# One Softplus in place of four operations and a sum, in the bidirectional scan of a four-layer kernel on one core

## The reference

```python
x_dbl = jnp.einsum('bkdl,kcd->bkcl', xs, x_proj_w)
dts, Bs, Cs = jnp.split(x_dbl, [R, R + N], axis=2)      # R = 8, N = 1
dts = jnp.einsum('bkrl,kdr->bkdl', dts, dt_w)
dt = jax.nn.softplus(dts + dt_b[None, :, :, None])
A = -jnp.exp(A_logs).reshape(K, Cm, N)
a = jnp.exp(dt[..., None] * A[None, :, :, None, :])      # the decay
b = (dt * u)[..., None] * Bs                             # the input term
h[l] = a[l] * h[l-1] + b[l]                              # the scan
ys = h * Cs + Ds * u
y02 = ys[:, 0] + ys[:, 2, :, ::-1]
y13 = ys[:, 1] + ys[:, 3, :, ::-1]
```

## Time and profile before

| what | value |
|---|---|
| median of the runs | 3650.93 us |
| profiled execution | 3652.96 us |
| its span in the profile | 3651.0 us |
| mean granted clock of PE | 0.937 |
| PE / DVE / ACT / POOL busy, of the span | 80 / 67 / 65 / 30% |

### The profile page before, as it was taken

One profiled execution on the slowest core, in us unless ns is written; L12 is line 12 of the kernel. 1 busy time (PEld: TensorE's weight loads), 2 busy tenths in 40 slices (PEclk: granted clock), 3 DMA queues, 4 the chain that ended last, 5 costly groups with the idle time before them and its releaser, 6 DMA issues. The chain is left out here.

```text
span 3651.0 us, 45449 instructions
## 1 busy us (share of the span) xinstructions
PE 2936.3 (80%) x17500; PEld 1593.8 (44%) x17500; DVE 2437.7 (67%) x2565; ACT 2368.8 (65%) x2681; POOL 1101.4 (30%) x612
## 2 busy tenths in 40 slices
PE   3688876969969877778996888776998788769699
PEld 2344335435534434434553433443555344354355
DVE  5787657865579657676466964768636886576761
ACT  2888545468689745437778864644868977454484
POOL 0236103642025500463103530146310453025430
PEclk9999998989999999899998999988999999989899
DMA  2001473500200157440020034643002005564101
GB/s 67 18 1 40 121 199 118 161 9 1 73 23 1 53 141 208 118 119 9 0 91 5 1 93 123 200 132 91 9 9 87 0 0 142 139 182 135 41 1 52
DMA packets 137227, 274.91 MB, mean 75 GB/s; under 512 B 17139, under 2 KB 93622, under 8 KB 137014
## 3 DMA queue, kind: packets, MB, share of 16 engines
q1 hardware_dynamic: 137014, 272.01, 26.7%
HBM read 194.07 MB, written 77.88 MB: 74 GB/s over the span
## 5 line engine op out<-in xcount | busy, mean ns | idle before, releaser
L1499 DVE SCALAR_TENSOR_TENSOR work<-region,cols,work 128x768 f32<-128x768 f32 x288 | 373.3, 1296 | 8.4 <-ACT work L902 3.3
L678 POOL TENSOR_TENSOR region<-region 128x768 f32<-128x768 f32 x96 | 225.4, 2352 | 350.6 <-ACT region L862 344.6
L1017 PE MATMUL psum<-region,m_fc 128*128 128x384 f32 x768 | 282.6, 491 | 11.8 <-ACT work L969 11.8
L1017 PE MATMUL psum<-region,m_cen 128*128 128x384 f32 x384 | 159.7, 541 | 158.8 <-DVE region L1613 60.9
L1270 PE MATMUL psum<-work,m_fc 128*128 128x384 f32 x768 | 282.3, 491 | 0.0
L654 POOL TENSOR_TENSOR work<-work,region 128x768 f32<-128x768 f32 x96 | 174.5, 1818 | 211.5 <-DVE work L1429 211.5
L642 POOL TENSOR_TENSOR work<-work 128x768 f32<-128x768 f32 x48 | 102.1, 2130 | 442.6 <-ACT work L783 416.1
L220 DVE SCALAR_TENSOR_TENSOR region<-region,cols 128x768 f32<-128x768 f32 x192 | 223.9, 1166 | 12.3 <-POOL region L678 8.3
L969 ACT ACTIVATE work<-psum,cols 128x768 f32<-128x768 f32 x192 | 173.1, 901 | 87.6 <-PE psum L1017 82.9
L1017 PE MATMUL psum<-work,m_avg 128*128 128x384 f32 x576 | 216.9, 500 | 16.0 <-ACT work L824 8.0
L1416 DVE SCALAR_TENSOR_TENSOR work<-region,cols,work 128x768 f32<-128x768 f32 x144 | 195.7, 1379 | 40.9 <-POOL work L642 37.5
(11 more groups left out here) (234 smaller groups left out, 7530.5 us busy)
## 6 DMA issues: line engine op xcount, KB each, us to landing
work<-scratch_cpe SPq DMA_DIRECT2D x192, 196.0 KB, 4.1
work<-scratch_dwc SPq DMA_DIRECT2D x192, 196.0 KB, 4.2
work<-scratch_lepe SPq DMA_DIRECT2D x192, 196.0 KB, 4.1
region<-in_tab_ch SPq DMA_DIRECT2D x48, 768.0 KB, 5.9
region<-in_x SPq DMA_DIRECT2D x48, 384.0 KB, 3.5
region<-in_tab_tok SPq DMA_DIRECT2D x48, 384.0 KB, 3.2
out<-work SPq DMA_DIRECT2D x48, 384.0 KB, 2.5
scratch_cpe<-region SPq DMA_DIRECT2D x44, 392.0 KB, 4.7
```

The source lines that it names most:

```text
L678: g.tensor_tensor(chain_tile(conv, n, p), chain_tile(conv, n - 1, p), chain_tile(conv, n, p), ALU.add).then_inc(tap_done[n], 1)
L1017: last = pe.matmul(psum[:, bank + s, 0:HC], weights[:, :], moving(s), start=(n == 0), stop=(n == len(terms) - 1))
L1499: v.scalar_tensor_tensor(out=by_row(tile(acc + p)), in0=prow(k, b, *TAPS[n]), scalar=tap_weight(conv, TAPS[n]), in1=by_row(tile(acc + p)), ...
```

## The change

Softplus becomes one ACT operation, `ACT.Softplus`, from PSUM to the tile. It is in another table set than Exp, so blocks are handled in pairs: load the one set, two Softplus, load the other, two decays. DVE's `step_size` goes. The banks are shared out anew: dt has only banks 0 and 1, B has banks 2 and 3 for even blocks and 4 and 5 for odd ones, C stays in 6 and 7. PE's stages become an order of six entries over pairs. DVE's stages all have lag 0. POOL issues `du` ahead of `add_y`. The backward outputs go to tiles 8 and 9 instead of 4 and 5, so that DVE waits for `add_y` two blocks back, where ACT's decay did.

```diff
-        bu_flat = psum[:, 4:6, :].rearrange("p a c -> p (a c)")[:, 0:BLK]
+        bu_flat = [psum[:, 2 + 2 * p:4 + 2 * p, :].rearrange("p a c -> p (a c)")[:, 0:BLK] for p in range(2)]
...
-                    g.tensor_tensor(y, y, tile(4 + p), ALU.add).then_inc(c["y"], 1)
-
-                chained(g, NB, [(2, add_y), (0, du)])
+                    g.tensor_tensor(y, y, tile(8 + p), ALU.add).then_inc(c["y"], 1)
+
+                chained(g, NB, [(0, du), (2, add_y)])
...
-                def soft(sweep, b, p):
+                def soft(sweep, g, _):
 
                     c = c_sets[sweep]
-                    a.wait_ge(c["dt"], done(i, b))
-                    scanned(a, i, sweep, "decay", b, 2)
-                    scanned(a, i, sweep, "du", b, 2)
-                    a.activation(halves(tile(p)), pair(2 * p), ACT.Abs, bias=col(f"l1_dtb{sweep}")).then_inc(c["abs"], 1)
-                    a.wait_ge(c["abs"], done(i, b))
-                    a.activation(tile(p), tile(p), ACT.Exp, scale=-1.0).then_inc(c["exp"], 1)
-                    a.activation(pair(2 * p), pair(2 * p), ACT.Relu, bias=col(f"l1_dtb{sweep}")).then_inc(c["relu"], 1)
-                    a.wait_ge(c["exp"], done(i, b))
-                    a.activation(tile(p), tile(p), ACT.Ln, bias=col("one")).then_inc(c["log"], 1)
-
-                def decay(sweep, b, p):
+                    a.preload_act_table_set("softplus")
+                    for p in range(2):
+                        b = 2 * g + p
+                        a.wait_ge(c["dt"], done(i, b))
+                        scanned(a, i, sweep, "decay", b, 2)
+                        scanned(a, i, sweep, "du", b, 2)
+                        a.activation(halves(tile(p)), pair(0), ACT.Softplus, bias=col(f"l1_dtb{sweep}")).then_inc(c["step"], 1)
+
+                def decay(sweep, g, _):
 
                     c = c_sets[sweep]
-                    a.wait_ge(c["step"], done(i, b))
-                    if sweep == 0 or is_first(b) or (isinstance(b, int) and b == 1):
-                        scanned(a, i, sweep, "hc", b, 2)
-                    else:
-                        a.wait_ge(c["y"], done(i, b - 2))
-                    a.activation(tile(4 + p), tile(p), ACT.Exp, scale=col(f"l1_A{sweep}")).then_inc(c["decay"], 1)
-
-                a.preload_act_table_set("natural_log_exp_and_others")
-                chained(a, NB, [(2, decay), (0, soft)])
+                    a.preload_act_table_set("exp_and_others")
+                    for p in range(2):
+                        b = 2 * g + p
+                        a.wait_ge(c["step"], done(i, b))
+                        scanned(a, i, sweep, "h", b, 2)
+                        a.activation(tile(4 + p), tile(p), ACT.Exp, scale=col(f"l1_A{sweep}")).then_inc(c["decay"], 1)
+
+                chained(a, NB // 2, [(0, soft), (0, decay)])
...
-                def dt(sweep, b, p):
-                    scanned(pe, i, sweep, "step", b, 2)
-                    product(2 * p, [(w_dt[sweep], flat_rows(2, sweep_block(sweep, b)))]).then_inc(c_sets[sweep]["dt"], 1)
...
+                def dt(p):
+                    def stage(sweep, g, _):
+                        b = 2 * g + p
+                        scanned(pe, i, sweep, "step", b, 1)
+                        product(0, [(w_dt[sweep], flat_rows(2, sweep_block(sweep, b)))]).then_inc(c_sets[sweep]["dt"], 1)
+                    return stage
+
+                def of_B(p):
...
+                        scanned(pe, i, sweep, "h", b, 2)
...
+                def of_C(p):
...
+                        scanned(pe, i, sweep, "hc", b, 1)
+                        product(6, [(w_C[sweep], flat_rows(2, sweep_block(sweep, b)))]).then_inc(c_sets[sweep]["C"], 1)
+                    return stage
 
                 all_done(pe, i, b_act)
-                chained(pe, NB, [(3, bc), (0, dt)])
+                chained(pe, NB // 2, [(1, of_C(0)), (0, dt(0)), (1, of_B(1)), (0, dt(1)), (1, of_C(1)), (0, of_B(0))])
...
-                    v.tensor_tensor(halves(tile(p)), halves(tile(p)), pair(2 * p), ALU.add).then_inc(c["step"], 1)
...
-                    y = flat(3, b) if sweep == 0 else tile(4 + p)
+                    if sweep == 1:
+                        v.wait_ge(c["y"], done(i, b - 2))
+                    y = flat(3, b) if sweep == 0 else tile(8 + p)
...
-                chained(v, NB, [(3, input_term), (3, scan), (3, outputs), (1, step_size)])
+                chained(v, NB, [(0, input_term), (0, scan), (0, outputs)])
```

More of the change, by code:

```diff
@@ L258, in build @@
             c_sets.append({k: signal(f"c{d}_{k}", o) for k, o in (
-                ("dt", "p"), ("B", "p"), ("C", "p"), ("abs", "a"), ("exp", "a"), ("relu", "a"), ("log", "a"), ("step", "v"),
-                ("decay", "a"),
+                ("dt", "p"), ("B", "p"), ("C", "p"), ("step", "a"), ("decay", "a"),
                 ("du", "g"), ("bu", "v"), ("h", "v"), ("hc", "v"), ("y", "g")) if d + k != "fy"})
@@ L1085, in middle, with stage @@
             def middle(i, following_runs):
-                def dt(sweep, b, p):
-                    scanned(pe, i, sweep, "step", b, 2)
-                    product(2 * p, [(w_dt[sweep], flat_rows(2, sweep_block(sweep, b)))]).then_inc(c_sets[sweep]["dt"], 1)
[L1090 to L1098, removed]
+                def dt(p):
[5 more added lines that the diff above has]
+                def of_B(p):
+                    def stage(sweep, g, _):
+                        b = 2 * g + p
+                        whole = flat(2, sweep_block(sweep, b))
+                        scanned(pe, i, sweep, "h", b, 2)
+                        pe.matmul(bu_flat[p][:, 0:BANK], w_B[sweep][:, :], whole[:, 0:BANK], start=True, stop=True)
+                        pe.matmul(bu_flat[p][:, BANK:BLK], w_B[sweep][:, :], whole[:, BANK:BLK], start=True, stop=True)\
+                            .then_inc(c_sets[sweep]["B"], 1)
+                    return stage
+                def of_C(p):
+                    def stage(sweep, g, _):
+                        b = 2 * g + p
+                        scanned(pe, i, sweep, "hc", b, 1)
+                        product(6, [(w_C[sweep], flat_rows(2, sweep_block(sweep, b)))]).then_inc(c_sets[sweep]["C"], 1)
+                    return stage
                 all_done(pe, i, b_act)
-                chained(pe, NB, [(3, bc), (0, dt)])
+                chained(pe, NB // 2, [(1, of_C(0)), (0, dt(0)), (1, of_B(1)), (0, dt(1)), (1, of_C(1)), (0, of_B(0))])
                 def yc(b, p):
@@ L1434, in input_term @@
                     v.wait_ge(c["B"], done(i, b))
-                    v.tensor_tensor(bu_flat, tile(2 + p), bu_flat, ALU.mult).then_inc(c["bu"], 1)
+                    v.tensor_tensor(bu_flat[p], tile(2 + p), bu_flat[p], ALU.mult).then_inc(c["bu"], 1)
                 def scan(sweep, b, p):
@@ L1443, in scan @@
                     way = (lambda ap: ap) if sweep == 0 else (lambda ap: ap[:, ::-1])
-                    v.tensor_tensor_scan(way(tile(6 + p)), way(tile(4 + p)), way(bu_flat), initial=start,
+                    v.tensor_tensor_scan(way(tile(6 + p)), way(tile(4 + p)), way(bu_flat[p]), initial=start,
                                          op0=ALU.mult, op1=ALU.add).then_inc(c["h"], 1)
```

## The result

The changed kernel took 3593.72 us (median of 4 runs, 3584.61 to 3595.31), the kernel before 3650.68 in the runs beside it. The ratio is 0.9837, with a 95% interval of 0.9822 to 0.9851: 57 us or 1.6% faster. The forecast was 3588.5 with a range of 3566 to 3628. The profiled execution was the fastest of the four, 3584.61 us, with a span of 3582.8.

What follows compares the result with a forecast made beforehand. DVE bounds the scan stage at 4.58 us a block; afterwards a DVE-PE ring of 8.10 a pair. Start 14.1 + 81.0 + end 9.7 = 104.8 against 120.4 an image, 62.4 us less in all: 3588.5 us, range 3566 to 3628.

Steps and rivals of the forecast that it cites:

- DVE bounds the stage: Layer 1 bidirectional scan before the change: DVE busy 102.68 of 105.00 us, 4.58 us a block with no gap.
- PE's floor of 7.74: PE's six products of 1.29 us per pair of blocks, the highest engine floor after the change.
- the ring of 8.10: Steady scan: C even, dt even, B odd, then DVE's odd input term, scan and outputs; 8.10 us a pair.
- ACT's ring: ACT's two Softplus, two decays, two loads and the wait for dt per pair: 7.85 us, margin 0.24.
- The Softplus at 0.90: One Softplus on ACT costs 0.90 us, taken from the Abs it replaces; upper bound 1.8.
- the loads at 1.28: Each table load on ACT lasts 1.28 us, two a pair, with no gap on either side.
- Rival 3: Loads hold ACT longer than 1.28; slower from a period of 9.5; with 1.4 extra, 3702 us; chance 0.07.
- rival 1: ACT's ring bounds because Softplus or an operation behind a load is dearer; 3604 to 3658 us; chance 0.17.
- Rival 2: PE waits less than counted, down to its 7.74 floor; 14 us less, 3574; chance 0.12.
- The start, 14.1: First Softplus to C of block 2: 12.8 us at full clock, 15.4 at PE's lower level; 14.1 taken.
- the end, 9.7: Last pair, without dt: DVE done at 7.8, POOL's last sum ends at 9.7 us.
- What follows moves up unchanged: DMA and stages behind the scan start from its end and move up with it; nothing else becomes late.

Runs made afterwards that it cites:

- e2: Changed kernel with PE issuing dt of the next even block ahead of C of the even block; 3580.41 us, ratio 0.9808 to the kernel before.
- e6: Kernel before with DVE's sum of Relu and Ln left out (step size wrong), banks and orders kept; 3636.65 us beside 3648.93, ratio 0.997.
- e3: Changed kernel with B back on one pair of banks (4 and 5), waiting for the previous block's scan; 3631.7 us, ratio 0.9956 to the kernel before.
- e8: Changed kernel with a third table load per pair, of a set with both Exp and Ln, before the odd decay; 3643.65 us, ratio 0.998.
- e1: The changed kernel run once more, unaltered; 3595.36 us, ratio 0.985 to the kernel before.
- e4: Changed kernel plus a second load of the same Exp set per pair, which was dropped, so the same program ran; 3593.32 us, ratio 0.9839.
- e5: Changed kernel with Abs in place of Softplus and no table loads in the loop (step size wrong); 3587.37 us, ratio 0.9825.
- e7: On top of e2, the second block's dt at an image's start goes to idle banks 4 and 5, not waiting for the first Softplus; 3575.21 us, ratio 0.9801.

## Why the prediction was right, step by step

**DVE bounds the stage, and the floor moves to PE.** Right, though PE's floor of 7.74 was reached in no run: first the ring of 8.10 and then, in e2, ACT's ring of 7.84 lay above it. There is an addition that the forecast did not have. e6 shows a second ring just beneath DVE's 4.58: B's single pair of banks, 4.53. The forecast counted the sum as 0.86 of 4.58 and the banks as a separate edit; it did not say that in the steady part the first is worth almost nothing without the second. e3 and e6, from the two sides, show this. At the start of a stage the shorter work is worth 18 us even with one pair of banks (e3).

**The Softplus at 0.90 and the loads at 1.28.** Right, and so was the choice of the trace over the Trainium skill's drain ("ScalarE: Activation LUTs", section "What ACT_TABLE_LOAD costs"): e8 shows 1.30 a load where ACT's ring bounds. Rival 3 is out, since no load drained the engine for longer, and so is rival 1, since no function was dearer. Its point of decision, a period of about 9.5, was real, though: e8 with 9.26 comes to within 0.2% of the kernel before. One reading was loose: the 0.83 that stands as Exp after Exp is from Ln to Exp in the earlier trace rows. Two decays together take the 1.76 that it gives.

**The ring of 8.10.** Right in size (8.10 in each profile of the kernel), and e2 shows that it is this ring: breaking it at C brought the period to 7.84, the 7.85 that was worked out for ACT. Rival 2, that PE waits less than counted, did not happen.

**The start, 14.1, and the end, 9.7.** Both came out a little shorter, and the stage's gain was 65.9 instead of 62.4. C of block 2 starts at 215.80 in image 0, 14.4 after the first Softplus, with PE at its lower clock. In images 1 and 2, where the granted clock is 1.00, the same subtraction (103.2 - 81.0 - 9.4) gives 12.8, the forecast's figure at full clock, and the first scan comes 5.80 after the first Softplus (forecast 5.76). The forecast took the middle of 12.8 and 15.4 for every image; in fact two images started at the one clock and two at the other. Its upper figure was too high, and its path at the lower clock was another one. In image 0 the first scan comes at 7.5, and it waited for dt 1, then B, then the input term, where the forecast had the load and the decay. The four starts together are 2.3 less than 4 x 14.1. The end is 9.4 in place of 9.7, because the sum has a slip: DVE is free at 11.82, which is 3.72 in the next period, but the last input term is put at 3.99. It is measured at 3.73 (300.53, with the last even C at 296.80).

**What follows moves up unchanged.** Here a little was lost, and 66 us of stage show as 57 in the medians. The span outside the four stages was 3169.5 before, and 3167.2, 3178.9 and 3177.3 in the three profiles of the changed program (the first, e1, e4), on the mean 5.0 more. The other 4 are no loss: the profiled execution before took 2.3 more than the median beside the result, and the three after took 1.9 less on the mean than the median of the changed kernel. Part of it is PE's clock at the start of the stage behind the scan. The stretches of 4 us from the end of the scan, image 0, first in the kernel before:
```profile
326.40:330.40 4.00, 2.25 (x4) 1.17 (x4) 1.94 (x2) 2.89 (x2) 0.03 (x1) 0.50 0.00 0
330.40:334.40 4.00, 3.10 (x10) 1.44 (x8) 1.01 (x1) 3.21 (x3) 0.00 (x0) 0.83 0.00 0
334.40:338.40 4.00, 2.73 (x9) 1.44 (x8) 1.87 (x2) 3.87 (x5) 2.02 (x1) 1.00 0.00 0
```
and in the changed kernel:
```profile
306.20:310.20 4.00, 2.27 (x4) 1.17 (x4) 1.94 (x2) 2.89 (x2) 0.00 (x1) 0.59 0.00 0
310.20:314.20 4.00, 3.10 (x5) 1.51 (x5) 1.01 (x1) 2.33 (x2) 0.00 (x0) 0.50 0.01 2
314.20:318.20 4.00, 3.10 (x6) 1.10 (x4) 1.71 (x2) 2.67 (x4) 0.67 (x1) 0.63 0.00 0
```
The number before the last two of each row is the granted clock. It rises in the second stretch before (0.83), and only in the third in the changed kernel (0.63); the last square of that stage starts 50.3 us after the scan's end before and 52.5 after. In the kernel before, two of the four images show the short form (clock up in the second stretch), in the changed kernel, e1 and e4 none of twelve, in e5 none of four, in e3 and e6 three of four each, in e2, e7 and e8 two, one and two of four. In the short form the last square is 50.3 to 50.6 behind the scan's end, in the long one 51.6 to 52.5, so the long form costs 1 to 2 us an image. Why it came more often in the changed kernel is not settled, and neither are the rest of the 5 us and the spread of 12 us between executions outside the stage.

## What to carry to other kernels

Work out every ring, not just each engine's load. An engine that is 98% busy can sit a twentieth of a microsecond above a ring through a single pair of banks, and then taking its work away brings next to nothing in the steady part until the banks are doubled (e6, e3). At the start of a stage, where blocks do not yet overlap, the same work may stand on the path, and there its removal pays by itself. So split a stage into start, steady part and end before you say where a gain came from. Where an engine whose program is in a fixed order must wait for another's result, put independent work directly ahead of the wait: one swapped entry brought 10 us of stage here (e2). A table load may stand in a loop if the ring through its engine has room for it; the margin read as "idle before, ended by PE" between the load and the next operation (0.24) told to a tenth what one more would cost.

## What the runs showed of the hardware

A switch of ACT's table set costs 1.28 us and at most 0.02 on either side, also where three loads of three sets stand in 9.26 us, 2.25 apart from the first to the second and from the second to the third (e8). Softplus takes 0.90 us from PSUM for 128 x 768 float32, as Abs does (e5). At the start of the scan PE's granted clock was 0.50 in some images and 1.00 in others of one execution. At 0.50 the second Softplus came 3.92 us after the first, at 1.00 2.55. Behind the idle stretch at the end of the scan PE works at its lower level, a granted clock of 0.50, and whether it comes back in the second or only in the third stretch of 4 us moved the last square of the next stage by 2 us (50.3 against 52.5).
